# Token, Mamba and expert block on one core: part tiles of delta and u stored with one transfer per kind in a part-major scratch layout, and the first group's last step copied from tile to tile

## The chip, the cores and the metric

One Trainium2 chip, one core, one launch. The metric is the time on the device in microseconds (us), as the median of several executions. TensorE is called PE, VectorE DVE, ScalarE ACT, GpSimd POOL, and SyncE, which here only issues DMAs, SP.

## The reference, cut to what matters

128 images become 5 tokens of 256 channels each (a patch convolution, local attention over windows, a class token). Then a Mamba layer runs over the 5 tokens in both directions and is added, and a gated expert layer is added. The change lies in the Mamba part:

```python
dt, Bm, Cm = (dbl[..., :r], dbl[..., r:r + n], dbl[..., r + n:])
delta = jax.nn.softplus(dt @ dt_w.T + dt_b)
A = -jnp.exp(A_log)
dA = jnp.exp(delta[..., None] * A)
dBu = delta[..., None] * Bm[:, :, None, :] * xc[..., None]
def step(h, inp):
    da, dbu, c = inp
    h = da * h + dbu
    return (h, jnp.einsum('bdn,bn->bd', h, c))
```

There are 128 images, 512 inner channels, 16 states, two directions. `u` stands for `delta * xc`.

## The kernel before, in words

**Two layouts.** The prepare stage works with 128 images on the 128 partitions. The scan works with (image, state) pairs on the partitions: a group is GB = 8 images times 16 states, and there are NG = 16 groups, taken in 8 pairs, one pair per turn of the loop on each engine (`pairs`, L1520). A float32 value of delta or u is split into three bfloat16 parts (high, middle, low) in `pt`, kept in a ring of NR = 3 slots. The parts go to the DRAM scratch `dparts` and `uparts` and come back per group as rows of `drows` and `urows`; PE then spreads the rows over the 16 states by a product with `selb` (`spread_delta`, L1680) or with the rows of B (`b_times_u`, L1686).

**Storing.** `prepare_vector` and `prepare_scalar` make ten items, `ITEMS` (L967), one for each direction d and scan step. `high` (L1212) and `middle` (L1221) on ACT and `low` (L1427) on DVE write an item's parts. `store(eng, n)` (L1003) waits for them and issues one DMA per kind (delta, u) and part. An item has 3 or 6 such DMAs of 128 rows of 1 KB. The scratch tensors are laid out (group, part and direction, image, step). Items 7 and 9 are stored by ACT (L1295, L1300), the others by SP. A slot of the ring is free when its stores have landed (`p_stored`).

**Loading.** `load_delta` (L1537) fetches the 6 part rows of the 8 images of one group, that is 48 partitions, with one DMA. `load_u` (L1542) fetches u with three DMAs, 6, 4 and 2 part rows per image (48, 32 and 16 partitions), because b is split into parts too. `load_b` (L1548) fetches 96 rows. A whole group (`load_rows`, L1551) is 192 KB of delta, 144 + 96 + 48 KB of u and 240 KB of b, in this order.

**SP's order in the prepare stage** is written out by hand in `prepare_sync` (L1556): stores of items 0 to 4, b of group 0, store 5, delta step 1 and u steps 1 and 2 of group 0, store 6, delta step 2 and u step 3, delta step 3, store 8, then b, u and delta of group 1, and, after everything is stored, the fourth step of delta for group 0 (L1600) and group 1 (L1601). PE waits for both of these ahead of its loop (L1752).

**SP's order in the loop** (`scan_sync`, body at L1644), for a pair i with groups 2i and 2i + 1: one slice of the expert weights and one of the output weights (L1641, L1637); when PE has spread group 2i (e_ready), `load_rows` of group 2i + 2; `store_y` of group 2i and of the second half of group 2i - 1 (L1606), each waiting for a copy by ACT (L1804); then `load_rows` of group 2i + 3, `store_y` twice, and four small stores (`store_k`, L1616). PE waits for all u and b rows of the next group ahead of its first `b_times_u` (L1765).

Of the kernel before, what the change touches and what calls it, by code (L numbers as in the profile page):

```python
# [16 lines left out]
BF16 = mybir.dt.bfloat16  # L17
# [11 lines left out]
L, DI, NS, R = 5, 512, 16, 16  # L29
ST = L - 1  # L30
DC = DI // P
NX = R + 2 * NS
GB = P // NS
NG = B // GB
# [16 lines left out]
KS = 12 * GB  # L51
# [25 lines left out]
def tower(nc, a, out):  # L77
    top = ExitStack()
    with top:
# [3 lines left out]
        def sem(name):  # L83
            return top.enter_context(nc.semaphore(name))
# [29 lines left out]
            return rows[:, VR[name]:VR[name] + n]  # L114


        dparts = nc.dram_tensor("dparts", (NG, 6, GB, ST * DI), BF16, kind="Internal").ap()
        uparts = nc.dram_tensor("uparts", (NG, 6, GB, (ST - 1) * DI), BF16, kind="Internal").ap()
        bparts = nc.dram_tensor("bparts", (NG, 12, GB, 2 * L * P), BF16, kind="Internal").ap()

        NY = 3 * 32 + GB
# [50 lines left out]
        gex = sb("gex", [P, W4, H], ctx=tok)  # L172

        s_vec, s_wall, s_proj, s_late = sem("s_vec"), sem("s_wall"), sem("s_proj"), sem("s_late")
        s_const, s_dtz = sem("s_const"), sem("s_dtz")
        s_bias, s_brow = sem("s_bias"), sem("s_brow")
        s_pairs, s_wmean, s_wready = sem("s_pairs"), sem("s_wmean"), sem("s_wready")
        x_landed = [[sem(f"x_landed{q}{c}") for c in range(EC)] for q in range(2)]
# [49 lines left out]
        def token_sync(sp):  # L228
            def load_x(w, c):
                src = a["xT"][:, w * WT + c * EN:w * WT + (c + 1) * EN]  # L230
                sp.dma_start(xbuf[:, w % 2, 0:KC - 1, c * EN:(c + 1) * EN],
                             src[0:(KC - 1) * P].rearrange("(k p) n -> p k n", p=P)).then_inc(x_landed[w % 2][c], 16)
                sp.dma_start(xbuf[0:KL, w % 2, KC - 1, c * EN:(c + 1) * EN],
                             src[(KC - 1) * P:KP]).then_inc(x_landed[w % 2][c], 16)

            for k in range(KC):
                if k % 2 == 0:
                    load_x_tile(sp, k)
                else:
                    load_conv_tile(sp, k)  # L240
            load_x(0, 1)
            load_x(0, 2)
            sp.dma_start(cols[:, :], a["vec_cols"]).then_inc(s_vec, 16)
            sp.dma_start(sel[:, :, :], a["sel"].rearrange("k (d m) -> k d m", d=2)).then_inc(s_vec, 16)
            sp.dma_start(wall[:, :, :], a["wall"].rearrange("(h p) n -> p h n", p=P)).then_inc(s_wall, 16)
            for c in range(EC):
                load_x(1, c)

            sp.dma_start(rows[:, :], a["vec_rows"].to_broadcast([P, NVR])).then_inc(s_proj, 16)
            for n, name in enumerate(["la_proj_w", "ga_proj_w", "mod_w"]):  # L250
                sp.dma_start(projw[:, n], a[name].rearrange("(h p) n -> p h n", p=P)).then_inc(s_proj, 16)
            for w in (2, 3):
                sp.wait_ge(emb_ready, 6 * (w - 1))
                for c in range(EC):
                    load_x(w, c)
            for d in range(2):
                sp.dma_start(inw[:, d], a["in_wT"][d].rearrange("(h p) n -> p h n", p=P)).then_inc(s_late, 16)
                sp.dma_start(xpw[:, d], a["xproj_wT"][d].rearrange("(c p) n -> p c n", p=P)).then_inc(s_late, 16)
                for g in range(GB):
                    sp.dma_start(expA[g * NS:(g + 1) * NS, d], a["A_logT"][d]).then_inc(s_late, 16)  # L260
            sp.dma_start(gatew[:, :, :], a["gate_wT"].rearrange("(h p) n -> p h n", p=P)).then_inc(s_late, 16)
            sp.wait_ge(s_dtz, 1)
            for d in range(2):
                sp.dma_start(dtw[0:R, d], a["dt_wT"][d]).then_inc(s_late, 16)
                sp.dma_start(dtw[32:33, d], a["dt_b"][d]).then_inc(s_late, 16)
            sp.wait_ge(s_late, LATE)

        def token_gpsimd(pool):
# [3 lines left out]
            pool.wait_ge(s_const, 3)  # L272
            pool.affine_select(out=ident[:, :], in_=ident[:, :], compare_op=ALU.not_equal, fill=1.0, base=0,
                               pattern=[[-1, P]], channel_multiplier=1).then_inc(s_const, 1)
            pool.memset(dtw[:, :, :], 0.0).then_inc(s_dtz, 1)

            pool.wait_ge(s_const, 4)
            for j in range(NG):
                pool.tensor_tensor(maskb[:, :, :], maskb[:, :, :],
                                   ident[:, j * GB:(j + 1) * GB].unsqueeze(2).to_broadcast([P, GB, NS]),  # L280
                                   ALU.add).then_inc(s_const, 1)
                pool.wait_ge(s_const, 5 + j)
            pool.wait_ge(s_vec, 32)
            pool.tensor_copy(selb[:, :, :], sel[:, :, :]).then_inc(s_const, 1)
            for w in range(W4):
# [621 lines left out]
        NR = 3  # L907
# [67 lines left out]

        def stores(n):
            lo_, hi_ = kinds(n)
            return 3 * (hi_ - lo_)

        def stored(r, n):  # L980
            return 16 * sum(stores(m) for m in range(r, n, NR))
# [21 lines left out]
        def store(eng, n):  # L1003
            d, r = ITEMS[n][0], n % NR
            lo_, hi_ = kinds(n)
            eng.wait_ge(hi_ready, n + 1)
            eng.wait_ge(mid_ready, n + 1)
            eng.wait_ge(low_ready, n + 1)
            for kind in range(lo_, hi_):
                o = (step(n) - 1 + kind) * DI  # L1010
                for k in range(3):
                    eng.dma_start((dparts, uparts)[kind][:, 2 * k + d, :, o:o + DI],
                                  pt[:, r, k, kind]).then_inc(p_stored[r], 16)

        def prepare_tensor(pe):
            def xi(n):
# [129 lines left out]
        def prepare_scalar(act):  # L1146
# [145 lines left out]
            middle(7)  # L1292
            high(8)
            silu_z(7)
            store(act, 7)  # L1295
            middle(8)
            act.activation(warm[:, 0:1], ident[:, 0:1], ACT.Exp, scale=-1.0)
            high(9)
            middle(9)
            store(act, 9)  # L1300

        def prepare_gpsimd(pool):
            pool.wait_ge(xnT_ready, 2)
# [183 lines left out]
        def y_sum(eng, d, t, done):  # L1487
            s_ = t if d == 0 else L - 1 - t
            eng.wait_ge(landing(d, s_), 48 if s_ == 3 else 96)
            eng.tensor_tensor(skip[:, d, t, :], skip[:, d, t, :], ytok[:, d, t, :], ALU.add).then_inc(done, 1)  # L1490

        d_landed, third_landed = [sem(f"d_landed{q}") for q in range(2)], sem("third_landed")
        early_landed = sem("early_landed")
        u_landed = [sem(f"u_landed{q}") for q in range(2)]
# [41 lines left out]

        def load_delta(sp, g, q, lo_, hi_, landed=None):  # L1537
            sp.dma_start(drows[KS // 2:KS, q, lo_ * DI:hi_ * DI],
                         dparts[bass.ds(g, 1), :, :, lo_ * DI:hi_ * DI].rearrange("g k i n -> (g k i) n")).then_inc(
                             landed or d_landed[q], 16)  # L1540

        def load_u(sp, g, q, lo_, hi_, landed=None):  # L1542
            for k, n in ((0, 6), (6, 4), (10, 2)):
                sp.dma_start(urows[k * GB:(k + n) * GB, q, lo_ * DI:hi_ * DI],  # L1544
                             uparts[bass.ds(g, 1), 0:n, :, lo_ * DI:hi_ * DI].rearrange("g k i n -> (g k i) n")).then_inc(
                                 landed or u_landed[q], 16)

        def load_b(sp, g, q, landed=None):  # L1548
            sp.dma_start(brows[:, q], bparts[bass.ds(g, 1)].rearrange("g k i n -> (g k i) n")).then_inc(landed or u_landed[q], 16)
# [6 lines left out]
        def prepare_sync(sp):  # L1556
# [26 lines left out]
            load_delta(sp, 0, 0, 0, 1)  # L1583
            load_u(sp, 0, 0, 0, 2, early_landed)
            store(sp, 6)
            sp.wait_ge(p_stored[0], stored(0, 7))
            sp.wait_ge(p_stored[2], stored(2, 7))
            load_delta(sp, 0, 0, 1, 2, u_landed[0])
            load_u(sp, 0, 0, 2, ST - 1)
            sp.wait_ge(p_stored[1], stored(1, 8))  # L1590
            load_delta(sp, 0, 0, 2, 3, third_landed)
            store(sp, 8)
            sp.wait_ge(z_ready, NI)
            load_b(sp, 1, 1)
            load_u(sp, 1, 1, 0, ST - 1)
            load_delta(sp, 1, 1, 0, 3)
            for r in range(NR):
                sp.wait_ge(p_stored[r], stored(r, NI))
            sp.wait_ge(skip_ready, NI)
            load_delta(sp, 0, 0, 3, ST)  # L1600
            load_delta(sp, 1, 1, 3, ST, d_landed[0])  # L1601

        def scan_sync(sp):
            def store_y(g, k):
# [74 lines left out]
        def scan_tensor(pe):  # L1679
            def spread_delta(g, q, j):  # L1680
                o = (j // 2) * DI
                pe.wait_ge(e_free, 8 * g + j + 1)
                pe.matmul(bank(j % 2), selb[:, j % 2, :], drows[:, q, o:o + DI],  # L1683
                          start=True, stop=True).then_inc(e_ready, 1)
# [47 lines left out]
                mm.then_inc(y_done[k], 1)  # L1732

            pe.wait_ge(cleared, 5)
            pe.wait_ge(s_const, 5 + NG)
            pe.wait_ge(d_landed[0], 16)
            pe.wait_ge(skip_ready, NI - 1)
            for j in range(2):
# [10 lines left out]
            pe.wait_ge(third_landed, 16)  # L1749
            for j in range(4, 6):  # L1750
                spread_delta(0, 0, j)
            pe.wait_ge(d_landed[0], 16 * 3)  # L1752

            def body(i, first, last):
                for q in range(2):
                    g = 2 * i + q
# [2 lines left out]
                    if first and q == 0:  # L1759
                        pe.wait_ge(z_copied, NI)  # L1760
                    b_times_u(g, q, 5)
                    spread_delta(g, q, 6)
                    spread_delta(g, q, 7)
                    if after:
                        pe.wait_ge(u_landed[1 - q], 64 * (i + q) + 64)  # L1765
                        b_times_u(g + 1, 1 - q, 0)
                        pe.wait_ge(d_landed[1 - q], 16 * (i + q) + (16 if q == 0 else 48))
                        spread_delta(g + 1, 1 - q, 0)
                        add_decayed(g)
                        spread_delta(g + 1, 1 - q, 1)  # L1770
# [526 lines left out]
```

## Time and profile before

| | us |
|---|---|
| median of 3 runs | 502.53 (500.88 to 507.13) |
| the profiled execution, its own time | 500.95 |
| span of its profile (first to last instruction) | 499.1 |
| PE busy in the span | 450.0 |
| DVE busy in the span | 372.3 |
| ACT busy in the span | 238.8 |
| token stage up to the first Mamba product | 0 to 205 |
| Mamba prepare stage | 205 to 290 |
| scan | 290 to 434 |
| finish | 434 to 499 |

The page gives busy time by engine. The stages are read from the lines of the chain of waits: L1020 begins at 205.42, the scan's first DVE product at 289.82, L2052 at 436.78. The median of the runs is 1.6 us above the profiled execution, and the span is 1.85 us below that execution's own time.

### The profile page before, as it was taken

What the parts mean: (1) busy time and instruction counts of PE and PEld (TensorE: products, weight loads), DVE (VectorE), ACT (ScalarE), POOL (GpSimd) and SP (SyncE); (2) the same over time, 40 slices, a digit from 0 to 9 for tenths busy, and PEclk for the clock granted to TensorE, in tenths of its full rate; (3) what the DMA queues carried; (4) which work ended last, traced back from release to release, by engine and by line L of the source; (5) the groups of instructions that cost most, each with busy time, mean ns of one, the idle gap of its engine ahead of it and who ended that gap; (6) DMA issues with size and microseconds to landing.
All of it is one profiled execution on the core that took longest, in us unless ns stands there. A gap on an engine that the chain in (4) does not pass through costs nothing.

```text
span 499.1 us, 6891 instructions
## 1 busy us (share of the span) xinstructions
PE 450.0 (90%) x1816; PEld 228.5 (46%) x1816; DVE 372.3 (75%) x709; ACT 238.8 (48%) x422; POOL 168.4 (34%) x164
## 2 busy tenths in 40 slices
PE   6999999999999989899969738988889889799997
PEld 3554655655555567577635402122222222285654
DVE  0256586566666668564999968899999999989756
ACT  1143423112212323365888855788888888531100
POOL 6000100100100020414430014889898989421000
PEclk9999999999999999996699967899999999999999
DMA  8992029200000000312035663466555655530000
GB/s 262 309 292 80 1 91 304 56 1 0 0 2 0 0 1 0 106 54 80 1 96 174 188 184 83 136 173 193 157 152 173 188 163 158 143 90 12 11 12 21
DMA packets 36344, 51.75 MB, mean 104 GB/s; under 512 B 5922, under 2 KB 26926, under 8 KB 36320
## 3 DMA queue, kind: packets, MB, share of 16 engines
q1 hardware_dynamic: 34736, 49.86, 34.0%
q10 hardware_dynamic: 1584, 1.59, 1.0%
q8 instruction: 12, 0.20, 0.2%
q14 instruction: 12, 0.10, 0.1%
HBM read 34.59 MB, written 16.52 MB: 102 GB/s over the span
## 4 chain that ended last, share of the span: by engine, by line
PE 65%; DVE 10%; SPq 8%; DMA 7%; issue 5%; ACT 3%; POOL 1%; DVEq 0%; POOLq 0%
PE ps L325 14%; PE ps L397 12%; PE ps L2085 7%; PE ps L1730 4%; PE ps L2052 4%; DMA brows<-bparts 4%; PE ps L1020 3%; PE ps L1683 3%; PE ps L1033 2%; DMA area<-in_xT 2%; PE ps L1696 2%; SPq L1544 2%; PE ps L1705 2%; PE ps L346 2%; PE ps L1065 2%
## 5 line engine op out<-in xcount | busy, mean ns | idle before, releaser
L1876 POOL TENSOR_TENSOR gb<-da,hb 128x512 f32<-128x512 f32 x62 | 77.7, 1275 | 61.1 <-ACT da L1796 54.2
L1796 ACT ACTIVATE da<-da 128x512 f32<-128x512 f32 x128 | 79.0, 629 | 25.0 <-DVE da L1907 20.9
L1907 DVE TENSOR_TENSOR da<-ps,expA 128x512 f32<-128x512 f32 x128 | 84.1, 685 | 8.0 <-PE ps L1683 7.2
L325 PE MATMUL ps<-area,convw 128*128 128x384 f32 (+1 forms) x220 | 73.4, 486 | 1.2 <-DMA area<-in_xT 1.2
L397 PE MATMUL ps<-wall,peT 128*128 128x512 f32 x144 | 67.7, 593 | 0.0
L1683 PE MATMUL ps<-drows,selb 96*128 96x512 bf16 x128 | 48.5, 401 | 11.7 <-DVE da L1907 5.1
L325 PEld LDWEIGHTS ps<-area,convw 128*128 128x128 f32 (+1 forms) x220 | 41.2, 190 | 29.0 <-DMA area<-in_xT 1.8
L1696 PE MATMUL ps<-urows,brows 96*128 96x512 bf16 x96 | 35.0, 394 | 13.9 <-DVE gb L1914 7.5
L582 ACT ACTIVATE kvs<-ps 128x512 f32<-128x512 f32 x36 | 21.5, 597 | 52.6 <-PE ps L397 52.6
L574 ACT ACTIVATE peT<-ps 128x384 f32<-128x384 f32 x24 | 11.8, 490 | 66.5 <-PE ps L325 59.3
L1683 PEld LDWEIGHTS ps<-drows,selb 96*128 96x128 bf16 x128 | 11.4, 98 | 61.9 <-DVE da L1907 50.1
L1876 POOL TENSOR_TENSOR gb<-da,gb 128x512 f32<-128x512 f32 x30 | 37.8, 1281 | 0.0
L1730 PE MATMUL ps<-gb,cst 128*8 128x512 f32 x256 | 34.0, 603 | 2.4 <-DVE gb L1969 1.5
L2085 PE MATMUL ps<-expw,xfT 128*128 128x512 f32 x76 | 34.2, 598 | 0.0
L688 DVE BATCH_NORM_STATS2 st<-ps 128x6 f32<-128x256 f32 x40 | 16.8, 429 | 21.7 <-PE ps L346 21.7
L397 PEld LDWEIGHTS ps<-wall,peT 128*128 128x128 f32 x144 | 24.5, 190 | 17.2 <-issue 17.2
L287 POOL TENSOR_TENSOR rstd<-veps,mhalf 128x1 f32<-128x1 f32 x4 | 2.2, 551 | 79.0 <-DVE veps L715 79.0
L1696 PEld LDWEIGHTS ps<-urows,brows 96*128 96x128 bf16 x96 | 9.1, 98 | 35.2 <-DVE gb L1914 21.3
L289 POOL TENSOR_TENSOR rstd<-veps,mhalf 128x9 f32<-128x9 f32 x4 | 7.2, 1806 | 51.5 <-DVE veps L736 51.5
L2178 DVE SCALAR_TENSOR_TENSOR mo<-ps,hot,mo 128x256 f32<-128x256 f32 x40 | 19.3, 484 | 5.5 <-PE ps L2085 4.1
L1914 DVE TENSOR_TENSOR gb<-da,ps 128x512 f32<-128x512 f32 x32 | 21.6, 676 | 1.9 <-ACT da L1796 1.9
L2085 PEld LDWEIGHTS ps<-expw,xfT 128*128 128x128 f32 x76 | 13.9, 190 | 14.8 <-issue 14.1
(246 smaller groups left out, 775.4 us busy)
## 6 DMA issues: line engine op xcount, KB each, us to landing
area<-in_xT SPq DMA_DIRECT2D x11, 768.0 KB
yscr<-yst SPq DMA_DIRECT2D x28, 208.0 KB
brows<-bparts SPq DMA_DIRECT2D x16, 240.0 KB, 3.0
drows<-dparts SPq DMA_DIRECT2D x14, 192.0 KB, 2.8
uparts<-pt SPq DMA_DIRECT2D x18, 128.0 KB, 2.4
dparts<-pt SPq DMA_DIRECT2D x18, 128.0 KB, 2.4
urows<-uparts SPq DMA_DIRECT2D x15, 144.0 KB, 2.7
inw<-in_in_wT SPq DMA_DIRECT2D x2, 1024.0 KB
```

Source lines behind the costliest of these rows:

```text
L325: mm = pe.matmul(bank(T_EMB + j % 2, 0, EN), convw[0:n, k, h * P:(h + 1) * P], xbuf[0:n, q, k, c * EN:(c + 1) * EN], start=(k == 0), stop= ...
L397: mm = pe.matmul(bank(T_KV + (q + t) % 2), peT[:, q, h, t * B:(t + 1) * B], wall[:, h, 512:1024], start=(h == 0), stop=(h == CH - 1))
L582: act.activation(kvs[:, q, t, :], bank(T_KV + (q + t) % 2), ACT.Copy).then_inc(kv_free, 1)
L1683: pe.matmul(bank(j % 2), selb[:, j % 2, :], drows[:, q, o:o + DI], start=True, stop=True).then_inc(e_ready, 1)
L1696: mm = pe.matmul(bank(b_), brows[:, q, o * P:(o + 1) * P], urows[:, q, v:v + DI], start=True, stop=lone, skip_group_check=True)
L1730: mm = pe.matmul(ps[32 * j:32 * j + GB, (6 + k) * 512:(7 + k) * 512], cst[:, q, d, token(s_, d), :], gb_at(q, 4 * k + j), start=True, stop ...
L1796: act.activation(da_at(q, j), da_at(q, j), ACT.Exp, scale=-1.0).then_inc(da_ready, 1)
L1876: pool.tensor_tensor(gb_at(q, j), da_at(q, j), state, ALU.mult).then_inc({2: m2_done, 3: m3_done, 4: m4_done}[s_], 1)
L1907: dve.tensor_tensor(da_at(q, j), bank(j % 2), expA[:, j % 2, :], ALU.mult).then_inc(e_free, 1)
L1914: dve.tensor_tensor(gb_at(q, d), da[:, d, :], bank(bu_bank(q, d)), ALU.mult).then_inc(bu_used, 1)
L2052: mm = pe.matmul(bank(2 + n % 2, 0, C), ygT[:, n % 2, d, c, :], outw[:, d, c, :], start=(d == 0 and c == 0), stop=(d == 1 and c == DC - 1))
L2085: mm = pe.matmul(bank(4 + m % 3), xfT[:, n % 2, h, :], expw[:, h, k * 512:(k + 1) * 512], start=(h == 0), stop=(h == CH - 1))
```

## The change

1. `dparts` and `uparts` are laid out (part and direction, group, image, step) instead of (group, part and direction, image, step).
2. `store` issues one DMA per kind with all three parts, 384 rows of 1 KB, so an item has 1 or 2 DMAs instead of 3 or 6. SP stores items 7 and 9 too; ACT issues none.
3. `load_delta` and `load_u` read the new layout. Their destinations stay 48, 48, 32 and 16 partitions; on the DRAM side the access now has 6, 6, 4 and 2 blocks of 8 rows.
4. The fourth step of delta of group 0 no longer goes through DRAM. `first_group_rows` copies it with 6 DMAs from the tiles `pt` to `drows` (8 partitions by 1 KB each) after the loads of group 1 and ahead of stores 8 and 9. PE waits for it just before `spread_delta(0, 0, 6)`, behind `b_times_u` 4 and 5, and for group 1's fourth step just before `spread_delta(1, 1, 6)`; the wait ahead of the loop is gone.
5. The load of delta for group 1 stands ahead of its b and u. SP also waits for e_ready 9 ahead of the last load of the prepare stage.
6. The semaphore `s_dtz` is merged into `s_const`.

```diff
-        dparts = nc.dram_tensor("dparts", (NG, 6, GB, ST * DI), BF16, kind="Internal").ap()
-        uparts = nc.dram_tensor("uparts", (NG, 6, GB, (ST - 1) * DI), BF16, kind="Internal").ap()
+        dparts = nc.dram_tensor("dparts", (6, NG, GB, ST * DI), BF16, kind="Internal").ap()
+        uparts = nc.dram_tensor("uparts", (6, NG, GB, (ST - 1) * DI), BF16, kind="Internal").ap()
...
             for kind in range(lo_, hi_):
                 o = (step(n) - 1 + kind) * DI
-                for k in range(3):
-                    eng.dma_start((dparts, uparts)[kind][:, 2 * k + d, :, o:o + DI],
-                                  pt[:, r, k, kind]).then_inc(p_stored[r], 16)
+                dst = (dparts, uparts)[kind].rearrange("(k d) g i n -> d (g i) k n", d=2)[d]
+                eng.dma_start(dst[:, :, o:o + DI], pt[:, r, :, kind, :]).then_inc(p_stored[r], 16)
+
+        def first_group_rows(eng, n):
+
+            d, r = ITEMS[n][0], n % NR
+            eng.wait_ge(hi_ready, n + 1)
+            eng.wait_ge(mid_ready, n + 1)
+            eng.wait_ge(low_ready, n + 1)
+            for k in range(3):
+                o = KS // 2 + (2 * k + d) * GB
+                eng.dma_start(drows[o:o + GB, 0, (ST - 1) * DI:ST * DI], pt[0:GB, r, k, 0]).then_inc(last_landed, 16)
...
-            store(act, 7)
...
-            store(act, 9)
...
-                         dparts[bass.ds(g, 1), :, :, lo_ * DI:hi_ * DI].rearrange("g k i n -> (g k i) n")).then_inc(
+                         dparts[:, bass.ds(g, 1), :, lo_ * DI:hi_ * DI].rearrange("k g i n -> (g k) i n")).then_inc(
                              landed or d_landed[q], 16)
...
-                             uparts[bass.ds(g, 1), 0:n, :, lo_ * DI:hi_ * DI].rearrange("g k i n -> (g k i) n")).then_inc(
+                             uparts[0:n, bass.ds(g, 1), :, lo_ * DI:hi_ * DI].rearrange("k g i n -> (g k) i n")).then_inc(
                                  landed or u_landed[q], 16)
...
             store(sp, 6)
+            store(sp, 7)
...
             load_delta(sp, 0, 0, 2, 3, third_landed)
-            store(sp, 8)
             sp.wait_ge(z_ready, NI)
+            load_delta(sp, 1, 1, 0, 3)
             load_b(sp, 1, 1)
             load_u(sp, 1, 1, 0, ST - 1)
-            load_delta(sp, 1, 1, 0, 3)
+            first_group_rows(sp, 8)
+            first_group_rows(sp, 9)
+            store(sp, 8)
+            store(sp, 9)
             for r in range(NR):
                 sp.wait_ge(p_stored[r], stored(r, NI))
             sp.wait_ge(skip_ready, NI)
-            load_delta(sp, 0, 0, 3, ST)
-            load_delta(sp, 1, 1, 3, ST, d_landed[0])
+            sp.wait_ge(e_ready, 9)
+            load_delta(sp, 1, 1, 3, ST)
...
-            pe.wait_ge(d_landed[0], 16 * 3)
-
             def body(i, first, last):
...
                     b_times_u(g, q, 5)
+                    if first:
+                        pe.wait_ge(*((last_landed, 16 * 6) if q == 0 else (d_landed[1], 16 * 2)))
                     spread_delta(g, q, 6)
```

## Rows read from the trace of the kernel before

**Rows 1.** Busy time by stretch: PE, PEld, DVE, ACT, POOL, clock, DMA share, GB/s
```profile
364.80:381.20 16.40, 14.41 (x74) 3.60 (x72) 16.05 (x26) 13.68 (x26) 14.92 (x13) 1.00 0.59 170
```
**Rows 2.** The chain of waits through one pair: start, us, what
```profile
358.04 3.46 DMA brows<-bparts
...
361.63 0.39 PE ps L1696
...
367.61 0.61 ACT yst L1804
...
368.36 0.34 SPq L1606
...
372.47 0.33 SPq L1538
...
374.44 3.53 DMA brows<-bparts
...
377.97 0.14 issue
```
**Rows 3.** Waits from 340 to 405 us
```profile
PE ps L1696 <- DMA brows<-bparts: 1.5, 4, 0.5
```
**Rows 4.** SP: its longest waits for ACT in the prepare stage, and its timeline
```profile
SPq L1008 <- ACT pt L1225: 22.2, 3, 18.3
...
278.89 1.83 SPq L1012 DMA_DIRECT2D dparts<-pt  x3
280.91 0.44 SPq L1538 DMA_DIRECT2D drows<-dparts  x1
289.14 0.32 SPq L1538 DMA_DIRECT2D drows<-dparts  x1
322.81 0.34 SPq L1538 DMA_DIRECT2D drows<-dparts  x1
```
**Rows 5.** Lines that issue DMAs: issue time min/median/max in ns; first and last
```profile
L231 SPq DMA_DIRECT2D area<-in_xT x11: 368/407/1070, 3.0 to 72.2; - x11
L1613 SPq DMA_DIRECT2D ytok<-yscr x8: 793/816/927, 426.4 to 435.5; - x8
L1534 SPq DMA_DIRECT2D ytok<-yst x6: 624/664/782, 423.0 to 437.1; - x6
L1538 SPq DMA_DIRECT2D drows<-dparts x20: 310/337/443, 280.9 to 411.0; - x20
...
DMA to landing us min/median/max: 1.8/2.8/3.9
L1012 SPq DMA_DIRECT2D uparts<-pt x18: 539/606/615, 251.9 to 286.2; - x18
```
**Rows 6.** Timeline of DVE, ACT and PE before the first group
```profile
293.02 0.69 DVE L1914 TENSOR_TENSOR gb<-da,ps 128x512 f32<-128x512 f32 x1 [1.92 <-ACT da L1796]
292.36 1.15 ACT L1796 ACTIVATE da<-da 128x512 f32<-128x512 f32 x2 [1.99 <-issue]
299.53 1.03 PE L1696 MATMUL ps<-urows,brows 96*128 96x512 bf16 x2 [3.11 <-DMA drows<-dparts]
```
**Rows 7.** Busy time by stretch, 32 to 45 us; last three: clock, DMA share, GB/s
```profile
32.00:33.00 1.00, 1.00 (x3) 0.19 (x1) 0.96 (x4) 0.00 (x0) 0.00 (x0) 1.00 1.06 401
...
40.00:41.00 1.00, 1.00 (x5) 0.58 (x4) 0.76 (x3) 0.60 (x1) 0.00 (x0) 1.00 0.26 92
...
44.00:45.00 1.00, 1.00 (x6) 0.52 (x4) 0.73 (x2) 0.60 (x1) 0.00 (x0) 1.00 0.27 97
```
**Rows 8.** The same view, where the granted clock falls
```profile
308.00:310.00 2.00, 1.13 (x4) 0.21 (x3) 2.00 (x4) 0.84 (x2) 1.58 (x2) 1.00 0.08 29
310.00:312.00 2.00, 1.78 (x5) 0.78 (x6) 2.00 (x5) 1.98 (x6) 2.00 (x2) 0.76 0.22 53
312.00:314.00 2.00, 2.00 (x7) 0.21 (x9) 1.08 (x2) 1.20 (x2) 2.00 (x3) 0.50 0.79 254
314.00:316.00 2.00, 2.00 (x16) 0.43 (x12) 1.46 (x4) 1.23 (x2) 1.84 (x2) 0.88 0.16 62
```

More of the change, by code:

```diff
@@ L174, in tower @@
         s_vec, s_wall, s_proj, s_late = sem("s_vec"), sem("s_wall"), sem("s_proj"), sem("s_late")
-        s_const, s_dtz = sem("s_const"), sem("s_dtz")
+        s_const = sem("s_const")
         s_bias, s_brow = sem("s_bias"), sem("s_brow")
@@ L261, in token_sync @@
             sp.dma_start(gatew[:, :, :], a["gate_wT"].rearrange("(h p) n -> p h n", p=P)).then_inc(s_late, 16)
-            sp.wait_ge(s_dtz, 1)
+            sp.wait_ge(s_const, 5)
             for d in range(2):
@@ L274, in token_gpsimd @@
                                pattern=[[-1, P]], channel_multiplier=1).then_inc(s_const, 1)
-            pool.memset(dtw[:, :, :], 0.0).then_inc(s_dtz, 1)
-            pool.wait_ge(s_const, 4)
+            pool.memset(dtw[:, :, :], 0.0).then_inc(s_const, 1)
+            pool.wait_ge(s_const, 5)
             for j in range(NG):
@@ L281, in token_gpsimd @@
                                    ALU.add).then_inc(s_const, 1)
-                pool.wait_ge(s_const, 5 + j)
+                pool.wait_ge(s_const, 6 + j)
             pool.wait_ge(s_vec, 32)
@@ L977, in stores @@
             lo_, hi_ = kinds(n)
-            return 3 * (hi_ - lo_)
+            return hi_ - lo_
         def stored(r, n):
@@ L1490, in y_sum @@
             eng.tensor_tensor(skip[:, d, t, :], skip[:, d, t, :], ytok[:, d, t, :], ALU.add).then_inc(done, 1)
+        last_landed = sem("last_landed")
         d_landed, third_landed = [sem(f"d_landed{q}") for q in range(2)], sem("third_landed")
@@ L1734, in scan_tensor @@
             pe.wait_ge(cleared, 5)
-            pe.wait_ge(s_const, 5 + NG)
+            pe.wait_ge(s_const, 6 + NG)
             pe.wait_ge(d_landed[0], 16)
@@ L1766, in body @@
                         b_times_u(g + 1, 1 - q, 0)
-                        pe.wait_ge(d_landed[1 - q], 16 * (i + q) + (16 if q == 0 else 48))
+                        pe.wait_ge(d_landed[1 - q], 16 if first and q == 0 else 16 * i + 32)
                         spread_delta(g + 1, 1 - q, 0)
```

## Prediction

> **What bounds the kernel now.** I read the busy times by stretch first, then the chain of waits, then SP's timeline, because the change touches only DMAs and their order. In a middle turn of the scan loop (16.4 us for a pair of groups) DVE is busy 16.05 us and PE 14.41 us at full clock [rows 1]. DVE looks like the bound, but the chain of waits does not run through it. One turn of the chain is a closed ring: b rows land at 361.50; PE works from 361.63 to 367.6; ACT copies y for 0.61; SP stores y at 368.36, issues four small stores and two weight loads and starts the next group's rows at 372.47; it issues their last DMA at 374.44; that lands 3.53 later, at 377.97 [rows 2]. So PE 6.1, ACT 0.6, SP 4.3 up to the load, and 5.5 from the start of the load to its landing make 16.5, the turn itself. There are five such landings on the chain (341.42, 358.04, 374.44, 390.90, 407.47; two are shown). PE's own wait there is small, 1.5 us over 4 turns [rows 3], since DVE is nearly as late. But small waits in a closed ring mean no slack for anything that is made longer. Whatever the new loads cost between 372.47 and 377.97 is paid once per turn.
>
> Ahead of the loop, PE waits 3.11 us for the fourth step of delta, until 299.53 [rows 6].
>
> **The change, part by part.** The sums are made against the profiled execution, 500.95 us; the median of the runs is 1.6 above it, and I add that at the end.
>
> *Stores.* An old store DMA (128 rows) takes 0.60 us to issue [rows 5]; 42 of them become 14. The nearest row for one with 384 rows in three dimensions on both sides is L231's (4 x 128 rows): 0.41, with 0.37 and 1.07 as ends [rows 5]. So item 6 costs SP 0.9 instead of 3.9, item 7 adds 0.4, and ACT loses two times three issues. Up to item 6 this lies beside other work: there SP waits for ACT, 22.2 us in three waits, not ACT for SP [rows 4]. It is worth nothing, and would cost something only if an issue took longer than the items are apart. One place is on the path: ACT's 1.99 of issuing ahead of the first exponential goes, so DVE's first state product, at 293.02 [rows 6], can be some 2 us earlier.
>
> *The loads before the loop.* SP is free for store 5 at 278.89 as before. One issue ends at 279.3. Then come four loads whose two sides no longer have the same shape (6 blocks of 8 rows against 48 partitions). Two lines of the trace issue such uneven DMAs, L1012 at 0.60 and L1613 at 0.82 (14 blocks against 112 partitions); even ones take 0.34 [rows 5]. I take 0.7, with 0.34 and 0.82 as ends. Four of them end at 282.4 where they ended at 282.8. Store 6 ends at 283.3, store 7 (its parts are ready at 284.2) at 284.6; 1.15 MB then land by about 286.7, where SP resumed at 289.14 [rows 4]. Four uneven loads end at 289.6 (before 290.9) and land at about 291.7 (before 292.2). Then delta step 3, delta of group 1, b (0.5) and three u loads: SP is through at 293.9. What is late next is the fourth step itself: six tile-to-tile copies of 8 rows. Such copies exist, L1534's, at 0.66 each [rows 5]; with gaps 4.2, to 298.1, and the shortest landing of a load, 1.8 [rows 5], gives 299.9. `spread_delta` 6 then starts there instead of after the two products that begin at 299.53, about 300.4. So this part gains 0.5: the copies skip a round trip through DRAM, but the queue of issues ahead of them is as long as the round trip was. Ends: -2.4 (copies issued at 0.34), +1.5 (uneven loads at 0.82 and a store at 1.07). DVE and ACT being ahead buys nothing more, since the arguments 6 and 7 wait for this.
>
> *The added waits.* Behind e_ready 9 on SP stand group 1's last load and then `load_rows` of group 2. PE makes that product some 2 us after 300, SP gets past it at 302, and the rows of group 2, needed at 310, are issued by 306 and land by 309. Nothing waits. The edit of `s_dtz` is in the first microseconds and costs nothing. Stores 8 and 9 are behind the copies and needed only by group 1's fourth step, some 8 us later.
>
> *The loads in the loop.* Here is the main term. The transfer time depends on how many of the 16 DMA engines serve it. Between 40 and 45 us all that is in flight are the 76-partition tails of the image tiles (L233). The DMA share stands at 0.26 to 0.27 in each of the five windows (two shown), at 92 to 97 GB/s [rows 7]: a quarter of the engines, 4 of 16, and 4 is the largest divisor of 76 up to 16. The loads now have 48, 48, 32 and 16 rows on both sides, so 16 engines each. After the change the outer count on the DRAM side is 6, 6, 4 and 2. If that count limits them, as 76 does, they run on 6, 6, 4 and 2 engines; if only the partitions count, on 16. I take the first.
>
> The Trainium skill has the rule in "DMA: Bandwidth & Descriptors", section "Why a DMA increments its semaphore by 16 and not by 1": a DMA issued by SP or ACT runs on the largest number of engines up to 16 that divides the slowest dimension of both sides, and on the lowest-numbered ones. The trace agrees for 76. By that rule the loads have 6, 6, 4 and 2 engines, which is what the sum below assumes anyway.
>
> The busiest engines, the first two, then carry 32 + 24 + 24 + 24 KB of delta and u and 15 KB of b: 119 KB a group, where each of 16 carried 42 KB. The fastest window gives 401 GB/s over 1.06 x 16 engines, 23.6 GB/s each [rows 7], so 119 KB take 5.2. The fixed part is a short load's 1.8 less its 0.15 of transfer, 1.65 [rows 5]. Together 6.8 from the start of the load to the landing of b, where it is 5.5 now: +1.3. The longer issues (4 x 0.36 = 1.4) lie beside this, as b's issue at +3.4 and its landing 2.6 to 3.0 later come to 6.0 to 6.4. Bounds per turn: 0 (16 engines, even issue) to +2.5 (both add up, since stores of y queue on the same engines).
>
> How often: the loads of the even groups 4 to 14, six turns. Group 2's has slack. Group 4's is issued from 322.81 [rows 4] and lands just as PE comes to it. The odd groups' loads start when PE frees the buffer, some 8 us ahead of need, against 6.8. The rest of the ring (PE, ACT, SP) is not made shorter by the delay, for PE works back to back in it. So 6 x 1.3 = +7.8. Busy engines: 2 x 119 KB and the y stores stay below a turn, so no second queue forms.
>
> *Sum.* 500.95 - 0.5 + 7.8 = 508.3; plus 1.6 for the median: **509.9**. A measurement of this kernel tells about 2% from no change, so this is within it, at +1.5%.
>
> **Rivals.**
> *A, the clock follows (slower).* PE stands still 1.3 us longer per turn. After PE was busy 1.13 of 2 us, the granted clock fell from 2.4 to 1.2 GHz and came back: 0.76, 0.50 and 0.88 in three stretches of 2 us [rows 8]. For: in the new turn the stretch before b lands (two spreads, then the wait) is as thin as the one ahead of that fall. Against: in the loop now, with shorter gaps, the clock holds at 1.00 [rows 1]. Place: the wait for b at L1765. It decides once b lands about 1 us later than now. Price: such a fall takes 2 x (0.24 + 0.50 + 0.12) = 1.7 us of full-speed work from PE, which is on the ring; six turns make 10: 520.
> *B, the DRAM side's count doesn't matter.* Loads stay on 16 engines. For: the rows and bytes of each load are the same. Against: rows 7. Issue that is 0.36 longer four times would be hidden only in part; with nothing lost, 502.5 - 0.5 = 502.0, and with copies issued at 0.34 it is 500.1.
> *C, the fourth step comes later than now.* SP has ten uneven or tile-to-tile issues ahead of it, and all are at the dear end: +1.5 instead of -0.5, so 511.9 with the main term. For: the queue on the first engines. Against: none of the issues in rows 5 has its maximum as a habit.
>
> **How the numbers follow.** Forecast (main term +0.8 to +1.8 a turn) 0.52; A 0.24; B 0.16; C 0.08. The forecast's own spread is 505 to 513, so a fifth of it is above 512.6, the 2% bound (0.10); so is nearly all of A (0.22) and half of C (0.04). Slower by over 2%: 0.36. Faster by over 2% means below 492.5, more than any sum above gives: 0.03. Within 2%: 0.61. The range takes in B's quick end and most of A: 499 to 522.
>
> **What would show it.** Right: PE's wait for b rows at L1696 grows from 0.4 to some 1.5 a turn; the loop's turn is 17.7 long; L1538 and L1544 issue at 0.6 to 0.8; b lands 6.5 to 7 after the load's first issue; DMA GB/s in the loop about 157 instead of 170; `spread_delta` 6 near 300. A is shown by a granted clock below 1.00 in the loop. Wrong: if the turn stays at 16.4, the engine count is not what I take it for; if the loads' landing is later and the turn still 16.4, the ring is not closed as I read it; if the fourth step lands before 298, the copies were mispriced.

## The result and the profile after

The changed kernel takes 536.5 us (median of 4 runs, 532.8 to 539.0), the kernel before in the same comparison 501.7 (500.1 to 507.1). The ratio is 1.069, interval 1.0645 to 1.0735. The forecast was 509.9 with a range of 499 to 522: the sign came out, the size did not. The profiled execution spans 535.0 us, 35.9 more than before, at a mean granted clock of 0.933 (before 0.965).

The page of the kernel after: busy times and the chain's shares.

```profile
span 535.0 us, 6871 instructions
...
PE 465.7 (87%) x1816; PEld 231.4 (43%) x1816; DVE 373.2 (70%) x709; ACT 240.0 (45%) x422; POOL 168.5 (32%) x164
...
PE 65%; SPq 11%; DMA 9%; DVE 7%; issue 4%; ACT 3%; POOL 1%; DVEq 0%; POOLq 0%
```

DVE has the same work as before, but SP's issuing and the DMAs hold 20% of the chain. Two middle turns of the loop by stretch (PE, PEld, DVE, ACT, POOL, clock, DMA share, GB/s), to set beside [rows 1]:

```profile
376.01:397.17 21.16, 16.15 (x73) 3.73 (x72) 16.24 (x27) 13.98 (x26) 14.92 (x13) 0.92 0.43 132
397.17:418.05 20.88, 16.14 (x73) 3.89 (x72) 16.22 (x27) 13.97 (x26) 14.91 (x13) 0.92 0.44 134
```

A turn takes 21 us instead of 16.4, with DVE still at 16.2: DVE is no longer near the bound. PE is busy 1.7 us longer for the same 73 matmuls, which is the clock at 0.92. The chain through one such turn (start, us, what) answers to [rows 2]:

```profile
397.17 4.53 DMA brows<-bparts
...
401.84 0.39 PE ps L1708
...
409.43 0.61 ACT yst L1816
...
410.32 0.31 SPq L1618
...
414.46 0.85 SPq L1546
...
415.52 0.76 SPq L1552
416.39 0.68 SPq L1552
417.17 0.68 SPq L1552
...
418.05 4.78 DMA brows<-bparts
```

It is the same closed ring (b's landing, PE, ACT's copy of y, SP's issues, the next load, b's landing), member by member. For the turn that ends with b's issue at 397.17 (its pieces: issue of b 376.01, PE 380.95, y copied 388.55, SP's store 389.44, load 393.58) and the turn 358.04 to 374.44 of before:

| member of the ring | before | after | predicted |
|---|---|---|---|
| b's issue to PE's first product | 3.59 | 4.94 | 2.7 to 3.5 |
| PE's part, to y's copy | 5.98 | 7.60 | 6.0 |
| y's copy to SP's store | 0.75 | 0.89 | unchanged |
| SP: stores and weights, to the load | 4.11 | 4.14 | unchanged |
| start of the load to b's issue | 1.97 | 3.59 | 3.4 |
| turn | 16.40 | 21.16 | 17.7 |

Three members grew: issue by 1.6, landing by 1.3 and PE by 1.6. The first two lie in one stretch, from the start of the load to b's landing: 5.5 before (372.47 to 377.97), 8.1 here (393.58 to 401.70), 6.8 predicted. In the six turns' other loads it is 8.4 to 9.3. ACT also copies the result tile k once per turn. By these copies six turns come out 30.8 us longer in all (4.4 to 6.3 each, against 1.3 predicted). The other 5.1 us arise ahead of the ring: y's first copy is at 308.25 instead of 305.76, that of the second half at 323.35 instead of 318.23.

PE's waits for b rows in the whole span (us in total, times, longest), beside [rows 3]:

```profile
PE ps L1708 <- DMA brows<-bparts: 22.8, 7, 4.0
```

The prediction's sign was a wait of some 1.5 a turn and 157 GB/s in the loop; it is over 3 a turn, and 132 to 134 GB/s.

Issue times of the loads and stores (min/median/max in ns, first and last), beside [rows 5]:

```profile
L1546 SPq DMA_DIRECT2D drows<-dparts x19: 724/802/1434, 281.1 to 440.8; - x19
L1552 SPq DMA_DIRECT2D urows<-uparts x51: 656/680/766, 282.1 to 443.5; - x51
L1012 SPq DMA_DIRECT2D dparts<-pt x8: 372/386/418, 258.0 to 302.0; - x8
...
DMA to landing us min/median/max: 2.5/2.9/5.0
L1012 SPq DMA_DIRECT2D uparts<-pt x6: 372/480/541, 252.0 to 284.8; - x6
```

The uneven loads issue at 0.80 (delta) and 0.68 (u), where they took 0.34 and 0.37 before, the merged stores at 0.39 and 0.48 (three of 0.60 before). The engine count shows in windows of 1 us behind a load of delta, which is issued at 393.58; the first load of u, with as many blocks, follows it and b's own issue is at 397.17 (columns as above):

```profile
395.00:396.00 1.00, 0.74 (x5) 0.21 (x9) 1.00 (x3) 0.43 (x2) 0.71 (x1) 1.00 0.34 46
396.00:397.00 1.00, 1.00 (x10) 0.21 (x3) 1.00 (x3) 0.70 (x2) 0.52 (x1) 1.00 0.37 143
397.00:398.00 1.00, 0.86 (x4) 0.19 (x2) 1.00 (x2) 0.66 (x2) 1.00 (x2) 1.00 0.38 144
398.00:399.00 1.00, 0.51 (x2) 0.10 (x1) 0.96 (x3) 1.00 (x3) 1.00 (x2) 1.00 0.80 195
```

In the first three the share stands at 0.34 to 0.38, about 6 of 16 engines (0.375), as it stood at 4 of 16 for 76 partitions [rows 7]. The Trainium skill's rule ("DMA: Bandwidth & Descriptors", section "Why a DMA increments its semaphore by 16 and not by 1") gives 6 for this load, from the slowest dimension on the DRAM side; by it the trace agrees. Two more things can be read here. The share does not drop from one load to the next, so as far as windows of 1 us tell these engines do not wait for an issue. And they do not move the same amount all the time: 46 GB/s in the first window, 8 or 9 for each busy engine, then 143 / (0.37 x 16) = 24 each.

And the clock, in stretches of 2 us across the wait for b:

```profile
397.00:399.00 2.00, 1.37 (x5) 0.29 (x3) 1.96 (x4) 1.66 (x4) 2.00 (x3) 1.00 0.59 170
399.00:401.00 2.00, 0.00 (x0) 0.00 (x0) 0.60 (x2) 1.27 (x3) 2.00 (x2) 1.00 0.76 261
401.00:403.00 2.00, 1.16 (x3) 0.73 (x4) 0.41 (x1) 0.00 (x0) 0.43 (x1) 0.80 0.38 143
403.00:405.00 2.00, 2.00 (x7) 0.27 (x9) 1.15 (x3) 1.23 (x2) 1.04 (x1) 0.50 0.70 180
405.00:407.00 2.00, 2.00 (x12) 0.31 (x4) 1.43 (x3) 1.23 (x2) 1.46 (x2) 0.85 0.21 78
```

PE stands idle through 399 to 401 and works on at 2.4 GHz for a moment when b lands; then the granted clock falls to 1.2 GHz (0.50) and is back at 1.00 by 407. The lost full-speed work is 2 x (0.20 + 0.50 + 0.15) = 1.7 us, the same as rival A's price. It falls on the products that the ring goes through. In two of the six turns the fall lasts longer. By the copies of k these two take 23.0 and 22.6 us, the other four 20.9 to 21.2, at a granted clock of 0.85 instead of 0.92; the first of the two:

```profile
343.15:366.18 23.03, 17.30 (x73) 4.17 (x72) 16.59 (x28) 13.97 (x25) 14.90 (x12) 0.85 0.41 127
```

In stretches of 2 us from 357 the clock is 0.71, 0.50, 0.50 and 0.59 there, which takes 3.4 us. Why it stays down for longer in these two is open; b's landing is no later after the load's start there (8.7 and 8.9) than in the turn with 9.3, whose fall is short.

Ahead of the first groups, PE's and then SP's timeline (start, us, instruction, idle time before it and what ended that), which answer to [rows 6] and [rows 4]:

```profile
294.75 0.61 PE L1695 MATMUL ps<-drows,selb 96*128 96x512 bf16 x1 [3.47 <-DMA urows<-uparts]
...
302.94 1.04 PE L1695 MATMUL ps<-drows,selb 96*128 96x512 bf16 x2 [3.90 <-DMA drows<-pt]
...
314.79 0.61 PE L1708 MATMUL ps<-urows,brows 96*128 96x512 bf16 x1 [1.78 <-DMA brows<-bparts]
```

```profile
289.83 0.79 SPq L1546 DMA_DIRECT2D drows<-dparts  x1
297.22 4.14 SPq L1022 DMA_DIRECT2D drows<-pt  x6
301.48 0.92 SPq L1012 DMA_DIRECT2D dparts<-pt  x2
305.20 1.63 SPq L1546 DMA_DIRECT2D drows<-dparts  x2
```

The six copies take SP 4.14 us, as the 4.2 of the prediction, but they begin at 297.22 and not 293.9. The two stores behind them take 3.2 us to land before SP may go on at 305.20, and group 2's rows, said to wait for nothing, then cost PE 1.78 us at 314.79.

### The profile page after: what moved, and what is told of

It reads as the page before. It is cut to its first block, busy times and chain, and to the rows that moved or that the text cites. A ratio compares the mean times of both kernels' runs of the same rounds, so it can differ in the third digit from the quotient of the medians.

```text
span 535.0 us, 6871 instructions
## 1 busy us (share of the span) xinstructions
PE 465.7 (87%) x1816; PEld 231.4 (43%) x1816; DVE 373.2 (70%) x709; ACT 240.0 (45%) x422; POOL 168.5 (32%) x164
## 4 chain that ended last, share of the span: by engine, by line
PE 65%; SPq 11%; DMA 9%; DVE 7%; issue 4%; ACT 3%; POOL 1%; DVEq 0%; POOLq 0%
PE ps L325 13%; PE ps L397 11%; DMA brows<-bparts 7%; PE ps L2097 6%; SPq L1552 4%; PE ps L1742 4%; PE ps L2064 3%; PE ps L1029 3%; PE ps L1717 2%; PE ps L1695 2%; PE ps L1042 2%; SPq L1546 2%; PE ps L1708 2%; PE ps L308 2%; PE ps L1074 2%
## 5 line engine op out<-in xcount | busy, mean ns | idle before, releaser
L1695 PE MATMUL ps<-drows,selb 96*128 96x512 bf16 x128 | 51.8, 427 | 15.7 <-DVE da L1919 5.0
L1708 PE MATMUL ps<-urows,brows 96*128 96x512 bf16 x96 | 36.8, 413 | 31.1 <-DMA brows<-bparts 22.8
L1742 PE MATMUL ps<-gb,cst 128*8 128x512 f32 x256 | 38.0, 669 | 2.4 <-DVE gb L1981 1.5
L1717 PE MATMUL ps<-gb,ident 128*128 128x512 f32 x30 | 22.0, 826 | 0.0
```

Source lines behind the costliest of these rows:

```text
L1708: mm = pe.matmul(bank(b_), brows[:, q, o * P:(o + 1) * P], urows[:, q, v:v + DI], start=True, stop=lone, skip_group_check=True)
L1717: pe.matmul(bank(4), ident[:, :], gb[:, 3, :], start=False, stop=True, skip_group_check=True).then_inc(h2_ready, 1)
L1742: mm = pe.matmul(ps[32 * j:32 * j + GB, (6 + k) * 512:(7 + k) * 512], cst[:, q, d, token(s_, d), :], gb_at(q, 4 * k + j), start=True, stop ...
```

## The experiments

The theory at the start: the part-major layout makes the loads uneven, they run on few DMA engines and issue slowly, the closed ring passes that on each turn, and the clock falls on top. The main rival: the new order (six copies, merged stores, added waits) costs the time and the layout does not. The code cuts are shortened: `a:b` stands for `lo_ * DI:hi_ * DI`, and the semaphore increments of some DMAs are left out.

**Layout alone.** The kernel before with the new layout and nothing else of the change:

```diff
-dparts = nc.dram_tensor("dparts", (NG, 6, GB, ST * DI), ...)
+dparts = nc.dram_tensor("dparts", (6, NG, GB, ST * DI), ...)
...
-    dparts[bass.ds(g, 1), :, :, a:b].rearrange("g k i n -> (g k i) n")
+    dparts[:, bass.ds(g, 1), :, a:b].rearrange("k g i n -> (g k) i n")
...
+sp.wait_ge(e_ready, 2)
 load_delta(sp, 0, 0, 3, ST)
```

uparts likewise; stores stay one per part. The added wait is one that is long over.

> The kernel before with the part-major scratch and the uneven loads alone; stores stay one per part, ACT stores items 7 and 9, the order and the fourth step's path are as before (only a wait for two products that are long done is added, for the semaphore). Theory 1 (the loads' form, through the closed ring): a turn of 20.5 to 21 us instead of 16.4, and 529 to 536 us in all. Rival (the order ahead of the loop, the merged stores and the copies are what costs): a turn near 16.4 to 17.7 and 502 to 512 us.

Measured: 534.3 us, ratio 1.067 (1.0637 to 1.0706). Four turns of 20.8 to 21.3 and two of 22.3 and 22.6. The layout with its uneven loads carries practically the whole loss.

**Order alone.** The changed kernel with the old layout, even loads and three stores per kind; the copies, the order of issues and the waits stay as changed.

```diff
-dparts = nc.dram_tensor("dparts", (6, NG, GB, ST * DI), ...)
+dparts = nc.dram_tensor("dparts", (NG, 6, GB, ST * DI), ...)
...
-    eng.dma_start(dst[:, :, o:o + DI], pt[:, r, :, kind, :])
+    for k in range(3):
+        eng.dma_start((dparts, uparts)[kind][:, 2 * k + d, :, o:o + DI], pt[:, r, k, kind])
```

> The changed kernel with the group-major scratch, the even loads and one store per part put back; the new order, SP's stores of items 7 and 9, the tile-to-tile copies and the moved waits stay. Theory 1: a turn of 16.4 us and 500 to 507 us, the fourth step being on time to within 3 us. Rival (order and copies cost): over 512 us, with PE waiting again at group 2 or for the copies.

Measured: 500.3 us, ratio 0.998 (0.9948 to 1.002). One of its ten executions took 2521.6 us, and nothing on record says why; the other nine lie between 496.8 and 502.9. One turn by stretch:

```profile
354.29:370.78 16.49, 14.51 (x73) 3.67 (x72) 16.12 (x27) 13.75 (x25) 14.89 (x13) 1.00 0.58 169
```

The turn is the old one, so the rival falls. Copies, order and waits are worth nothing that can be measured with single stores; the merged stores are tested further down.

**Is it a ring?** The kernel before, with four small DMAs to a scratch tensor that nobody reads, ahead of the loads of even groups.

```diff
 sp.wait_ge(e_ready, 8 * g + 8)
+if q == 0:
+    for k in range(4):
+        sp.dma_start(ring[bass.ds(i, 1), k], ident[0:GB, :])
 load_rows(sp, g + 2, q)
```

> The kernel before with four small stores of 8 rows on SP just ahead of the loads of each even group, about 4 x 0.46 = 1.8 us of issue per turn and hardly any bytes. If the ring PE, ACT, SP, load is closed without slack, the turn grows by 1.6 to 1.9 us (more if PE's clock falls) and the time by 10 to 13 us, to 512 to 515. If DVE sets the turn and SP has slack, less than 0.5 a turn and at most 505 us.

Measured: 513.0 us, ratio 1.026 (1.0218 to 1.0307). Its chain:

```profile
364.68 2.92 DMA brows<-bparts
...
367.74 0.39 PE ps L1702
...
373.71 0.61 ACT yst L1810
...
378.57 0.31 SPq L1660
...
380.49 0.34 SPq L1538
...
382.56 2.70 DMA brows<-bparts
```

The four issues push the load back by 1.92 us (378.57 to 380.49), and the turn grows by 1.48, from 16.40 to 17.88, a little under the 1.6 expected. What did not come through is in the landing, 2.92 instead of 3.46. I read it so that what is queued ahead of b drains while SP issues; no view shows this by itself. So the ring is closed, with some 0.4 us of give. In other turns (19.3 to 20.2) the clock fell as well.

**The clock's share.** The changed kernel, with three products into a free bank ahead of PE's wait for the rows. Nobody reads them; they only keep PE busy.

```diff
+if q == 1:
+    need(pe, y_copied[2], i)
+    for _ in range(3):
+        pe.matmul(bank(5), ident[:, :], siluz[:, 0, 0, :], start=True, stop=True)
 pe.wait_ge(u_landed[1 - q], 64 * (i + q) + 64)
```

> The changed kernel with three float32 products into a free bank (no result is used) just ahead of PE's wait for the b rows of each even group, so that PE is busy while it would wait 3.3 us. If the fall of the granted clock is a cost of its own (PE's part of the ring took 7.6 us instead of 6.0), the turn falls from 20.9 to 19.3 to 19.8 and the time by 6 to 11 us against the changed kernel, to 525 to 530. If the clock costs nothing, the time stays at 534 to 538 or grows.

Measured: 523.9 us, ratio 1.045 (1.0405 to 1.0503), 12.6 less than the changed kernel.

```profile
368.06:387.69 19.63, 16.96 (x79) 4.72 (x78) 16.14 (x27) 13.76 (x26) 14.95 (x13) 1.00 0.47 142
```

The clock stays at 1.00 and the turn is 19.6 instead of 21. In its chain PE's part goes from 373.10 to 379.06, 5.96 us, as before the change. More work on PE made the kernel faster. Of the 22.9 us that are left over the kernel before (501.0 in this comparison), 19.3 lie in the six turns, whose PE part is as before: this is the stretch from the load to b's landing.

**Engine count apart from issue time.** The kernel before, with the loop's load of delta in two even pieces: 46 + 2 rows. The control is 32 + 16, with the same number of DMAs and bytes.

```diff
-load_delta(sp, g, q, 0, ST)
+src = dparts[bass.ds(g, 1)].rearrange("g k i n -> (g k i) n")
+sp.dma_start(drows[KS // 2:KS // 2 + 46, q, :], src[0:46]).then_inc(d_landed[q], 16)
+sp.dma_start(drows[KS // 2 + 46:KS, q, :], src[46:KS // 2]).then_inc(u_landed[q], 16)
 load_u(sp, g, q, 0, ST - 1)
```

> The kernel before; in the loop the 192 KB of delta rows are loaded by two DMAs of 46 and 2 partitions, both of one shape on either side. Its pair is the split into 32 and 16 partitions, with the same issues, rows and bytes. By the count rule (largest divisor up to 16) 46 and 2 partitions have 2 engines each, 32 and 16 have 16. Theory 1: the few engines cost by themselves: 96 KB on each of two engines is some 4 us, so b lands 2 to 3.5 us later than in the pair, the turn grows by that and the time is 12 to 25 us above the pair's. Rival (only the longer issue of uneven shapes costs, the engine count does not): the same as the pair within 1%.

> The control: delta rows by two DMAs of 32 and 16 partitions. One more issue of 0.34 plus a gap on the ring, 0.45 a turn: by the closed ring 502 + 6 x 0.45 = 505 us. If SP has slack, 502.

Measured: 533.4 us, ratio 1.064 (1.0568 to 1.0713), against 502.6 us, ratio 1.002 (0.9987 to 1.0056), for the control. The chain of the 46 + 2 kernel:

```profile
397.87 0.39 PE ps L1698
...
405.48 0.61 ACT yst L1806
...
410.35 0.26 SPq L1553
...
410.80 0.26 SPq L1554
...
412.67 6.89 DMA brows<-bparts
```

and of the control:

```profile
391.30 0.33 SPq L1553
...
393.76 3.29 DMA brows<-bparts
```

The 46 rows issue as fast as the control's (0.26), b is issued 2.32 us after the load's start (control 2.46), and it lands 6.89 later instead of 3.29. 46 has no divisor up to 16 above 2, 32 and 16 have 16. Half a microsecond of this landing shows what is left in flight:

```profile
417.00:417.50 0.50, 0.00 (x0) 0.00 (x0) 0.00 (x0) 0.20 (x1) 0.50 (x2) 1.00 0.12 47
```

PE and DVE stand still, and the DMA share is 0.12, which is 2 engines of 16. So the number of engines alone costs 31 us, more than the 12 to 25 expected. The clock's fall that follows from the wait is in this: PE's part of the turn is 7.61 here too (397.87 to 405.48), where it was 5.98. It costs this much with a load whose two sides have the same shape and an ordinary issue time. It also does so with the scratch laid out as before. The changed layout puts the six blocks of a group 512 KB apart in DRAM, which would be a rival of its own; the 46 + 2 kernel loses as much without it, and the six engines of the changed kernel reach 24 GB/s each, as the engines of [rows 7] do. The control shows the other thing too: 0.49 more of issue (2.46 for 1.97) moved the turn from 16.40 to 16.50 only, since b landed sooner after it; by a ring without any give I had expected 505.

**Taking the loads out of the ring.** The loads of the even groups are issued ahead of the last stores of y and of k, in the kernel before and in the changed one.

```diff
 store_y(g, 0)
+if q == 1 and more:
+    sp.wait_ge(e_ready, 8 * g + 16)
+    load_rows(sp, g + 3, 0)
 if not (first and q == 0):
     store_y(g - 1, 1)
```

> The kernel before with the loads of each even group issued ahead of the second store of y and the four small stores, so that the loads no longer wait for ACT's copy: the ring is opened. The load then starts when PE frees the buffer, some 2.5 us earlier. Theory 1: PE's waits for b rows (1.5 us in 4 turns) vanish and DVE (16.05 of 16.4) sets the turn: 16.1, so 499 to 501 us. Rival (the chain through SP is only one of two equal ones, or y stores that come later hold ACT): no change or up to 505.

> The changed kernel with the same move. Opening the ring takes away ACT, y store, four small stores and the weights, 4.3 to 5 us, from the path to the even groups' loads. Theory 1 (the uneven loads cost because the ring is closed): the turn falls from 20.9 to 17 to 18.5 and the time to 510 to 520. Rival (the first two DMA engines or the landing itself bound it, wherever the load stands): 530 or more.

Measured: 500.2 us, ratio 0.998 (0.994 to 1.0014), and 516.9 us, ratio 1.030 (1.0238 to 1.0367). A turn of each, the kernel before first:

```profile
372.57:388.84 16.27, 14.51 (x76) 3.62 (x72) 16.02 (x27) 13.72 (x27) 14.95 (x13) 1.00 0.56 172
```

```profile
386.98:405.50 18.52, 14.41 (x73) 3.63 (x72) 16.02 (x27) 12.99 (x26) 14.74 (x13) 1.00 0.49 150
```

In the kernel before, the ring was only 0.13 us above the next bound: without it DVE is busy 16.02 of 16.27 us. In the changed kernel the move returns 20 of 35 us. The loads do not wait for y any more, but now they are a ring by themselves: PE frees the rows, the load starts at 383.34, b lands at 391.91, 8.6 later, and PE and DVE need 9.9 until the next start at 401.86.

**Order alone with that move.** The second experiment and the move together.

> The order, the copies and the moved waits of the change with the group-major scratch and even loads, plus the loads of even groups ahead of the second y store and the four small stores. If the two small gains (each within noise by itself: 0.9984 and 0.9977) add, the ratio to the kernel before is 0.994 to 0.997 and the turn 16.26. Rival: both gains were chance of the runs, ratio 0.998 to 1.003.

Measured: 499.2 us, ratio 0.995 (0.9929 to 0.9974), with turns of 16.26. The two gains, each within the noise by itself, add up to one that is clear of it, though far below 2%.

**Merged stores with even loads.** One store per kind asks that the parts can be reached by one regular pattern; the layout need not be part-major for that. Here it is (group, image, part, step), and the rows of the selection matrix follow that order.

```diff
-dparts = nc.dram_tensor("dparts", (6, NG, GB, ST * DI), ...)
+dparts = nc.dram_tensor("dparts", (NG, GB, 6, ST * DI), ...)
...
-dst = (dparts, uparts)[kind].rearrange("(k d) g i n -> d (g i) k n", d=2)[d]
+dst = (dparts, uparts)[kind].rearrange("g i (k d) n -> d (g i) k n", d=2)[d]
...
-drows[o:o + GB, 0, (ST - 1) * DI:ST * DI]
+drows[o:KS:6, 0, (ST - 1) * DI:ST * DI]
...
+sel = sel.transpose(2, 0, 1, 3, 4, 5)
```

Delta and the 48-row load of u are then even; the loads of 32 and 16 rows stay uneven, with 8 as their outer count.

> The changed kernel, its stores with all parts in one DMA kept, but with the scratch laid out (group, image, part, step) and the rows of delta, u and b in that order on the partitions (the selection matrix is reordered to suit). Delta and the first u load are then contiguous 48 rows on both sides: 16 engines and an even issue. The other two u loads are uneven, 8 blocks of 4 and of 2 rows: 8 engines. Theory 1 (cost follows the engine count and the uneven issue): the busiest engines carry 54 KB instead of 119 (42 before), issue grows by 0.7, the turn is 16.9 to 17.8 and the time 502 to 510 us. Rival (the merged stores are what costs): 525 or more.

> The same with the loads of even groups ahead of the second y store and the four small stores. With the ring open, 1 us of longer loads is hidden: turn 16.26 to 16.4, 497 to 503 us. Rival (ring is not what passes it on): as the kernel without the move, 502 to 510.

Measured: 503.0 us, ratio 1.005 (1.0032 to 1.0073); with the loads moved ahead 497.9 us, ratio 0.993 (0.9894 to 0.9966), turns of 16.26 to 16.27 behind a first one of 16.40. The end of one turn of the first:

```profile
389.26 0.34 SPq L1546
...
389.78 0.33 SPq L1552
...
390.22 0.76 SPq L1552
...
391.08 0.69 SPq L1552
...
391.98 3.25 DMA brows<-bparts
```

Its two uneven issues make 2.72 from load to b's issue instead of 1.97, its b lands about as soon as before, and its turn is 17.23 instead of 16.40 (17.0 to 17.3 in the others): here 0.75 of issue costs 0.8. The second kernel has the lowest median of the study: the merged stores and the copies kept, the uneven issues out of the ring. Against the kernel before it gains 0.7%; its interval overlaps that of the order alone with the same move (0.995), so which of the two is better is not shown.

## Why the prediction was wrong

*The reading of the kernel was right.* The loop is a closed ring through b's landing, PE, y and SP; the rows of before showed it, and the kernels with four small DMAs and with the loads moved ahead confirm it. The outer count on the DRAM side does limit the engines (rival B falls: windows at 0.34 to 0.38 behind the load). That the stores, the copies and the added waits are worth about nothing holds too: 500.3 for the order alone, 503.0 with merged stores and the big loads even.

*"Together 6.8 from the start of the load to the landing of b" failed.* This is the main term, and it was put too low. The stretch took 8.1 to 9.3, so the turn pays 2.6 or more for it and not 1.3. The prediction had 1.65 fixed and 5.2 for 119 KB on each of the first two engines, at 23.6 GB/s. With the same fixed part 119 KB took 6.5 in the shortest case (393.58 to 401.70), 19 GB/s as a mean. The 46 + 2 kernel, whose first two engines carry 92 + 4 + 18 + 15 = 129 KB, took 9.2 (410.35 to 419.56): 17.5 GB/s. The rate of an engine that runs was right: 24 GB/s each in two of the windows above. What the term left out is the time in which these engines are busy and move little, as in the window of 46 GB/s at the start of delta. It also left out that delta's own issue (0.85 for 0.33) is ahead of its first byte. How the missing 1.3 divides between these two, and whether the stores of y on the same engines add to it, was not separated. (Each of 16 engines carried 45 KB before the change, not 42; the sum does not use this.)

*"The longer issues lie beside this" came out, on weak grounds.* The issue was sized well, 3.59 as against 3.4. I took b's landing as 2.6 to 3.0 after its own issue, where the ring of before has 3.46 and 3.53 [rows 2]. With these the way over the issue is 3.59 + 3.5 = 7.1, and the busiest engines, at 8.1, are still the later of the two. The 46 + 2 kernel says the same: b is issued after 2.32, as with the old loads, and lands after 9.2. So the 1.6 of issue and the 1.3 of landing in the table are two pieces of one stretch and not two causes. My outer bound, +2.5 "since both add up", comes close to the 2.6 by its size and not by its reason. Where no engine is crowded, the issue does decide: in the kernel with two uneven issues 0.75 of issue costs 0.8 of turn.

*Rival A was not a rival.* I held the clock's fall against the main term, with a chance of 0.24, although I wrote that it follows once b lands 1 us later. In the event it came with the main term and on top of it, in every turn. Its place (the wait for b) was right. Its price (1.7) was right in four turns: 1.7 by the windows, 1.6 in PE's part of the ring; in the other two it was 3.4. The filler kernel, whose clock stays at 1.00 in its turns, needs 118.4 us for the six turns instead of 129.8. Had I added what I had priced, +2.5 and +1.7 a turn, six turns would have made 25 us, and the forecast 527.

*"Nothing waits" behind e_ready 9 failed.* Group 2's rows are behind the two stores, whose landing SP waits for. I placed these stores "behind the copies and needed only by group 1's fourth step", and so counted for that step alone; but all that SP issues later is behind the same wait. They landed at 305.20, b of group 2 was issued at 309.04, behind uneven loads, and landed 5.71 later. PE waited 1.78 us, and the ring of the next groups began that late.

*The fourth step was mistimed.* It was to be 0.5 us early and is some 2.5 late: `spread_delta` 6 at 302.94. The copies cost what I had said. SP reached them 3.3 us later than I had it, since it resumed its loads at 289.83 and not at 286.7. Of these 3.1 us, 1.9 are the start of item 6's store of u (284.82), for in this execution all of the stage was already 1.7 us late, with one more fall of the clock at 259. The other 1.2 are its landing, 5.0 where I had allowed 3.8. The first part is of one execution, and nothing shows that the change caused it. Rival C had the direction of this part and a size too small; the order-alone kernel, at 500.3, shows that with even loads and single stores nothing of it is left to see.

*Why the range didn't hold it.* It reached to the main term or to A, never to both, and the main term was half its size. Not tried: uneven loads on all 16 engines, which would show the issue time apart from the engines at its full size.

## What to carry to other kernels

Before a scratch layout is turned for the sake of its writers, look at what its readers become: write down for each load the outermost dimension on both sides, its largest divisor up to 16, and the bytes of the busiest engine. The landing of the last load is the later of two: its own issue and its landing time as the ring shows it, or the time of the busiest engine from the first issue on, with some margin over its bytes at full rate (119 KB took 6.5 us here, not 5.2). To this add the clock's fall if the new idle time is of the kind before which the trace already shows a fall; the delay and the fall are terms of one sum and not alternatives. Look also at what the queue waits for ahead of the next load, be it only the landing of a store. A layout that serves both sides may exist: here (group, image, part) kept the merged stores and left the big loads on 16 engines.

## What the runs showed of the hardware that I had not expected

- Splitting two rows off a load of 48 costs 6%: with 46 + 2 rows the kernel takes 533.4 us, with 32 + 16 it takes 502.6, with the same bytes, the same number of DMAs and no longer issue (0.26 for 0.33).
- An uneven load costs 0.68 to 0.85 us to issue, hardly less for few rows (0.68 for 16 rows in 2 blocks and for 32 in 4, 0.76 for 48 in 6), an even one 0.34 to 0.37. The merged store with three dimensions on both sides costs only 0.37 to 0.54.
- Three products that nobody reads, in a wait of PE, made the kernel 12.6 us faster, for the clock stayed at 2.4 GHz.
- b's landing has some give: with 1.92 more of issue ahead of it, it came 0.5 sooner after its own issue. On 6 and on 2 engines the busiest engine set the landing, and b's own issue did not.
- The same wait can cost the clock 1.7 or 3.4 us: in two of six turns the granted clock was down for twice as long as in the others, and why is open.
